# The steps' softplus chunk by chunk in the state-space stage of a perceiver kernel

## The reference, cut to what matters

```
ssm = x @ W_x.T
ts, Bm, Cm = (ssm[..., :R], ssm[..., R:R + N], ssm[..., R + N:])
ts = rms_forward(ts); Bm = rms_forward(Bm); Cm = rms_forward(Cm)
dt = jax.nn.softplus(ts @ W_dt.T + b_dt)
A = -jnp.exp(A_log)
def step(state, inp):
    dA = jnp.exp(dt_t[..., None] * A)
    state = state * dA + (dt_t * u_t)[..., None] * B_t[:, None, :]
    y = jnp.einsum('bdn,bn->bd', state, C_t)
```

## Time and profile before

| | us |
|---|---|
| median of three runs (2577.83 to 2579.14) | 2577.83 |
| the profiled execution, its device time | 2577.61 |
| its span, first to last instruction | 2575.7 |
| TensorE busy in the span | 2475.4 (96%) |
| VectorE busy | 1857.3 (72%) |
| ScalarE busy | 1525.6 (59%) |
| GpSimd busy | 1464.5 (57%) |

### The profile page before, as it was taken

One profiled execution on the slowest core, in us unless ns is written; L12 is line 12 of the kernel. 1 busy time (PEld: TensorE's weight loads), 2 busy tenths in 40 slices (PEclk: granted clock), 3 DMA queues, 4 the chain that ended last, 5 costly groups with the idle time before them and its releaser, 6 DMA issues. The chain is left out here.

```text
span 2575.7 us, 42761 instructions
## 1 busy us (share of the span) xinstructions
PE 2475.4 (96%) x16984; PEld 2271.0 (88%) x16984; DVE 1857.3 (72%) x2085; ACT 1525.6 (59%) x2605; POOL 1464.5 (57%) x1201
## 2 busy tenths in 40 slices
PE   8999999999999999999999999999999699899889
PEld 6899999999999999999999999999887477754557
DVE  4157787787877788778877778877746699843573
ACT  3356665676566666667666566665643577622672
POOL 3345686586666568657666756865700499400452
PEclk9999999999999999999999999999999799999889
DMA  6511011111111101112111120111251300188200
GB/s 224 193 60 54 29 62 54 43 59 54 37 49 46 62 29 62 54 36 66 54 37 38 50 68 29 62 29 33 102 188 54 131 1 1 54 315 310 84 2 17
DMA packets 112238, 188.70 MB, mean 73 GB/s; under 512 B 9940, under 2 KB 74836, under 8 KB 110252
## 3 DMA queue, kind: packets, MB, share of 16 engines
q1 hardware_dynamic: 103724, 177.64, 20.6%
q10 hardware_dynamic: 8320, 8.39, 1.0%
HBM read 165.98 MB, written 20.02 MB: 72 GB/s over the span
## 5 line engine op out<-in xcount | busy, mean ns | idle before, releaser
L513 POOL TENSOR_TENSOR xa_pt_lo<-xs_st,xa_pt_hi 128x1024 fp32r<-128x1024 f32 x191 | 468.4, 2484 | 466.3 <-ACT xa_pt_hi L767 466.3
L59 PE MATMUL ctx_kv_ps<-ctx_wv_hi,ctx_hi 128*128 128x256 f32 x1536 | 431.7, 281 | 1.8 <-DVE xa_v_lo L880 1.8
L60 PE MATMUL ctx_kv_ps<-ctx_wv_lo,ctx_hi 128*128 128x256 f32 x1536 | 430.0, 280 | 0.0
L61 PE MATMUL ctx_kv_ps<-ctx_wv_hi,ctx_lo 128*128 128x256 f32 x1536 | 429.9, 280 | 0.0
L59 PE MATMUL ctx_kv_ps<-ctx_hi,ctx_wk_hi 128*128 128x402 f32 (+1 forms) x1024 | 357.3, 349 | 1.8 <-DVE xa_k_lo L873 1.8
L60 PE MATMUL ctx_kv_ps<-ctx_lo,ctx_wk_hi 128*128 128x402 f32 (+1 forms) x1024 | 353.2, 345 | 0.0
L61 PE MATMUL ctx_kv_ps<-ctx_hi,ctx_wk_lo 128*128 128x402 f32 (+1 forms) x1024 | 353.0, 345 | 0.0
L59 PEld LDWEIGHTS ctx_kv_ps<-ctx_wv_hi,ctx_hi 128*128 128x128 f32 x1536 | 288.6, 188 | 2.2 <-DVE xa_v_lo L880 2.2
L60 PEld LDWEIGHTS ctx_kv_ps<-ctx_wv_lo,ctx_hi 128*128 128x128 f32 x1536 | 289.4, 188 | 0.0
L61 PEld LDWEIGHTS ctx_kv_ps<-ctx_wv_hi,ctx_lo 128*128 128x128 f32 x1536 | 288.5, 188 | 0.0
L744 ACT ACTIVATE xs_st<-xs_s_ps 128x512 f32<-128x512 f32 (+1 forms) x448 | 263.3, 604 | 29.1
(11 more groups left out here) (531 smaller groups left out, 6765.8 us busy)
## 6 DMA issues: line engine op xcount, KB each, us to landing
ctx_raw<-in_ctx_t SPq DMA_DIRECT2D x24, 804.0 KB, 6.9
ctx_wk_raw<-in_xa_wk SPq DMA_DIRECT2D x64, 256.0 KB, 2.8
ctx_wv_raw<-in_xa_wv SPq DMA_DIRECT2D x32, 512.0 KB, 4.4
n_back<-in_ctx SPq DMA_DIRECT2D x8, 1280.0 KB, 10.4
q_raw<-in_xa_wq SPq DMA_DIRECT2D x8, 1024.0 KB, 4.9
q_scratch<-q_q_sb ACTq DMA_DIRECT2D x8, 1024.0 KB, 4.4
ctx_q_raw<-q_scratch SPq DMA_DIRECT2D x64, 128.0 KB, 2.7
o_scratch<-xa_o_sb SPq DMA_DIRECT2D x64, 128.0 KB, 1.7
```

The source lines that it names most:

```text
L59: nc.tensor.matmul(out, left[0], right[0], start=first, stop=False)
L60: nc.tensor.matmul(out, left[0], right[1], start=False, stop=False)
L61: return nc.tensor.matmul(out, left[1], right[0], start=False, stop=last)
L513: nc.gpsimd.tensor_tensor(by_chunk(pt_lo, p), scored(j, p).rearrange("p g q c -> p g c q"), by_chunk(pt_hi, p).bitcast(F32), ALU.subtract) ...
```

## The change

The logarithm of chunk c - 2 is issued behind the exponential of chunk c - 1, inside the loop over the chunks; the addition of chunk c - 4 is issued in VectorE's loop at chunk c; the exponential of A_log is issued at chunk 1, and its negation at chunk 4. One logarithm of a 128 x 1 tile (`logs`) is new, ahead of the loop.

```diff
-        eps_sb = sc.sb("eps", [P, 1])
+        eps_sb, logs = sc.sb("eps", [P, 1]), sc.sb("logs", [P, 1])
...
+            def step_sum(c):
+                dve.wait_ge(d_read, c + 1)
+                dve.wait_ge(ln_set, c + 1)
+                nc.vector.tensor_tensor(dt_sb[:, c, :], dt_sb[:, c, :], work[:, c, :], ALU.add).then_inc(dt_set, 1)
+
             for c in range(DC):
                 if folded_pair(c):
                     for n in range(HN):
...
                 dve.wait_ge(d_abs, c + 1)
                 nc.vector.tensor_scalar(work[:, c, :], d_ps[:, c % 4, :], bd[:, c:c + 1], 0.0,
                                         ALU.add, ALU.max).then_inc(d_read, 1)
-            for c in range(DC):
-                dve.wait_ge(d_read, c + 1)
-                dve.wait_ge(ln_set, c + 1)
-                nc.vector.tensor_tensor(dt_sb[:, c, :], dt_sb[:, c, :], work[:, c, :], ALU.add).then_inc(dt_set, 1)
-            dve.wait_ge(a_exp, 1)
-            nc.vector.tensor_scalar(a_sb[:, :, :], a_sb[:, :, :], -1.0, None, ALU.mult)
+                if c == 4:
+                    dve.wait_ge(a_exp, 1)
+                    nc.vector.tensor_scalar(a_sb[:, :, :], a_sb[:, :, :], -1.0, None, ALU.mult)
+                if c > 3:
+                    step_sum(c - 4)
+            for c in range(DC - 4, DC):
+                step_sum(c)
...
             nc.scalar.activation(steps_t[:, :], t_ps[0:COPIES * RANK, :], ACT.Copy).then_inc(steps_set, 1)
+            nc.scalar.activation(logs[:, :], eps_sb[:, :], ACT.Ln, bias=1.0)
             act.wait_ge(small_in, (COPIES + 1) * 16)
 
             def decline(c):
                 act.wait_ge(d_abs, c + 1)
                 nc.scalar.activation(dt_sb[:, c, :], dt_sb[:, c, :], ACT.Exp, scale=-1.0).then_inc(e_set, 1)
 
+            def logarithm(c):
+                act.wait_ge(e_set, c + 1)
+                nc.scalar.activation(dt_sb[:, c, :], dt_sb[:, c, :], ACT.Ln, bias=1.0).then_inc(ln_set, 1)
+
             for c in range(DC):
                 act.wait_ge(d_full, c + 1)
                 nc.scalar.activation(dt_sb[:, c, :], d_ps[:, c % 4, :], ACT.Abs, bias=bd[:, c:c + 1]).then_inc(d_abs, 1)
+                if c == 1:
+                    act.wait_ge(scan_in, 32)
+                    nc.scalar.activation(a_sb[:, :, :], a_sb[:, :, :], ACT.Exp).then_inc(a_exp, 1)
                 if c > 0:
                     decline(c - 1)
+                if c > 1:
+                    logarithm(c - 2)
             decline(DC - 1)
-            for c in range(DC):
-                act.wait_ge(e_set, c + 1)
-                nc.scalar.activation(dt_sb[:, c, :], dt_sb[:, c, :], ACT.Ln, bias=1.0).then_inc(ln_set, 1)
-            act.wait_ge(scan_in, 32)
-            nc.scalar.activation(a_sb[:, :, :], a_sb[:, :, :], ACT.Exp).then_inc(a_exp, 1)
+            logarithm(DC - 2)
+            logarithm(DC - 1)
```

## The result

| | before | changed |
|---|---|---|
| median of five runs, us | 2577.95 | 2590.67 |
| range of the runs, us | 2577.83 to 2579.14 | 2589.76 to 2596.11 |
| profiled execution: device time, span | 2577.61, 2575.7 | 2595.96, 2594.0 |

The change makes the kernel 12.7 us slower by the medians. The ratio goes by all runs and not by the two medians: it is 1.0055, with a 95% interval of 1.0044 to 1.0066, and the means of the five and five runs are 14.3 us apart. The forecast was 2592.8 in a range of 2589 to 2597.

The account below looks back on a forecast made before the run. VectorE's end, behind ScalarE's chain, was taken to bound the steps' stage. The stage 14.5 us longer plus 0.5 at the scan's start made 15.0 us, so 2592.8 us, range 2589 to 2597.

Parts of the forecast that it names:

- cost at the scan's start: Load between the zeros' copy and the scan's exponentials: first scan 2.96 instead of 2.45 us behind GpSimd's product, 0.5 more.
- small logarithm on the path: New small logarithm and its load, some 1.28 + 0.2 us, lie in ScalarE's 2.22 us wait for the first product: cost 0.
- What a load costs: Each table load in a row of ScalarE's work costs 1.41 us, with 1.28 as the lower end.
- The stage: The steps' stage, up to GpSimd's first scan product, becomes 14.5 us longer, with ScalarE's last logarithm late at the end.
- The gain of the order by itself: In the steps' stage and scan's start, interleaving by itself gains about 3.3 us against 18.3 for added loads.
- that one sentence: Sum counted by loads: 13 more on the path at 1.41 make 18.3 us, and interleaving by itself gains about 3.3.
- Behind it the scan should read as before: After the first scan, nothing takes the delay in and the scan's profile stays as before.
- rival 3: TensorE's clock changes VectorE's 2.58 us wait in the scan: coming twice 2595.4 us, removed 2590.2; 9% together.
- Rivals 1 and 2: 1: one table set serves both functions, 2575.1 us, 3%; 2: alternating tables cost a second pause per load, 2609.4 us, 2%.

Follow-up runs that it names:

- the pairs: Changed kernel with its loop's logarithms issued in pairs at chunks 3, 5 and 7, 27 table loads instead of 33: median 2584.34 us, ratio 1.0022.
- the kernels with one table: Logarithms replaced by same-shape exponentials, 18 table loads: in the changed kernel ratio 0.9988, in the kernel before 0.9997, there with the table loaded early 0.9985.
- the changed order with one table: Changed kernel with its eight logarithms and the small new one replaced by exponentials, 18 table loads instead of 33: median 2575.63 us, ratio 0.9988.
- the order of before with A_log's part alone: Kernel before with only A_log's exponential moved to chunk 1 and its negation to VectorE's chunk 4: median 2577.78 us, ratio 0.9997.
- the second comparison: The changed kernel run once more, unaltered, beside new runs of the kernel before: median 2594.02 us, ratio 1.0056.

## Why the prediction was right

Its steps against the profile, counted from the first absolute value:

| step | predicted | measured |
|---|---|---|
| loads in the stage, at the scan's start | 16, 1 | 16, 1 |
| from one logarithm to the next | 4.44 | 4.46 |
| last logarithm ends | 33.04 | 33.14 |
| last addition ends | 33.99 | 34.01 |
| GpSimd's first product of the scan | 34.32 | 34.37 |
| first scan | 37.28 | 37.25 |
| cost at the scan's start | 0.51 | 0.43 |
| small logarithm on the path | 0 | 0 (0.71 us of the wait left) |

*What a load costs.* 1.41 us was taken from two places of the trace of before; six loads less in the pairs gave 1.42, and the load ahead of the additions 1.43. That the built program's loads are what runs was the step on which the sign hung, and the kernels with one table show that it is these loads and nothing else in the new order.

*The stage.* +14.50 predicted, 34.37 - 19.87 = +14.50 measured. The gain of the order by itself was put at 3.3 us as a remainder of the sum. The experiments give the interleaving itself nothing (19.66 against 19.71). The remainder is two other things. VectorE ended 3.64 us behind the last logarithm before (2043.59 against 2039.95) and ends 0.87 behind it now, so that 2.8 us of ScalarE's longer chain cost nothing; and the scan's load costs 0.43 instead of 1.41. The 0.2 of A_log's exponential goes the other way. The sum was right, since it walked ScalarE's chain from start to end and did not multiply loads; that one sentence in it was not. On VectorE two details were wrong and cost nothing: beside GpSimd's product a chunk's diagonal matrices, maximum and addition take 1.90 + 0.75 + 0.68 = 3.33 us and not under 3, of the 4.46 there are; and VectorE waits ahead of its maxima, not ahead of most additions.

*Behind the scan's start.* "Behind it the scan should read as before" did not hold, and it is the one step that failed: 1.0 us comes back there. SyncE's transfer at the start of the next stage:

```profile
2240.24 0.33 SPq L2285 DMA_DIRECT2D mo_raw<-in_fl_w  x1
```

From the first value to it it takes 214.82 us against 200.91 before, +13.91, while the first scan stood at +14.93. All of it comes back by the seventh scan, which starts 17.28 us behind the first instead of 18.27. The second scan before, then in the changed kernel:

```profile
2048.68 2.30 DVE L2042 TENSOR_TENSOR_SCAN ms_h_ps<-ms_h_ps,mamba_a_d_bu 128x1024 f32<-128x1024 f32 x1
```

```profile
2064.88 2.27 DVE L2055 TENSOR_TENSOR_SCAN ms_h_ps<-ms_h_ps,mamba_a_d_bu 128x1024 f32<-128x1024 f32 x1
```

Before, the second and third scan start 2.31 us apart, at the pace of GpSimd's products (2.32 each). Now the first scan has waited longer for ScalarE, GpSimd is ahead, and they start 2.21 and 2.18 apart. So 0.23 of the 0.43 us that the load costs at the scan's start are given back at once. The rest is VectorE's wait ahead of the seventh scan, 1.84 us instead of 2.58, and it goes with the granted clock. Before (two stretches, the first scan at 2046.37):

```profile
2050.00:2056.00 6.00, 3.35 (x14) 2.44 (x13) 5.99 (x4) 3.99 (x8) 6.00 (x4) 0.50 0.06 25
2056.00:2060.00 4.00, 4.00 (x26) 3.48 (x25) 4.00 (x3) 2.16 (x4) 4.00 (x2) 0.75 0.00 0
```

And changed (the first scan at 2062.67):

```profile
2066.00:2072.00 6.00, 3.61 (x15) 2.69 (x14) 6.00 (x4) 3.95 (x8) 6.00 (x4) 0.50 0.06 22
2072.00:2074.00 2.00, 2.00 (x14) 1.64 (x13) 2.00 (x2) 1.97 (x4) 2.00 (x2) 0.87 0.00 0
```

The mean of 0.75 over four us before puts the rise from 1.2 to 2.4 GHz near 2058, 11.6 us behind the first scan; the mean of 0.87 over two us puts it near 2072.5 now, 9.8 behind. This is the better half of rival 3, which expected up to 2.6 us. The first turnings at the lower level are the same in both (1.97 us), so the difference lies in when the rise comes. The same reading of all eleven profiles goes with this, though no run moves the rise by itself: the rise comes 9.8 to 12.4 us behind the first scan and the seventh scan 17.3 to 18.7 us behind it, and where the one is later, so is the other (a single pair of neighbours is exchanged, by 0.11 us). Whether the change moves the rise is open. The changed kernel has it at 9.8 and 10.0 in its two profiles, but the changed order with one table, which idles less than before, has it at 10.2, and the order of before with A_log's part alone at 10.7. So it varies without the loads too.

*The median.* 15.0 us were predicted. The first comparison has 12.7 by the medians and 14.3 by the means; the second has 15.0 by the medians (2594.02 less 2579.00) and 14.4 by its ratio of 1.0056. With the 13.9 us between the first value and the next stage all of these agree within the spread of the runs, which in the changed kernel reaches 6.4 us. So the times of whole runs don't confirm the sum to better than some 2 us, and that the second comparison hits it is luck; what bears it out is the table above. The profiled execution was forecast at 2592.6 and took 2595.96, 18.35 us more than before: 1.37 stand ahead of the first value, 13.91 between it and the next stage, and 3.01 behind (347.59 against 344.58), which the second profile of the same kernel (344.34) does not show. The lower bound of the range was added up wrongly: 2590.6 less rival 3's 2.6 is 2588.0, not 2588.9. The measured median lies above both.

*Rivals 1 and 2.* With exponential and logarithm in turn each needed its own load, so one table did not serve both. The Trainium skill (ScalarE: Activation LUTs, Table sets: the hidden batching unit) has a set with both of them, for one load; the trace does not agree, since in this built program each switch has its own. Whether that set exists and was not chosen, no run here shows. No load had a second pause behind it in the stage, in this kernel or in those of the experiments (0.01 to 0.02 us between a load in a row of work and its activation); the drain of 1380 ns in the Trainium skill (ScalarE: Activation LUTs, What ACT_TABLE_LOAD costs) shows in none.

## What to carry to other kernels

Before two functions are interleaved on ScalarE, count the table loads in the built program, which the source does not show, and price each by its place: about 1.4 us where ScalarE's chain sets the end, 0.4 at the scan's start beside GpSimd's product, nothing where ScalarE waits or where another engine is later. If a chain of several functions is the bound, look for a formula with fewer of them before reordering: here, with z small enough for it, it gained 8.0 us of the stage and 6 to 8 of the whole (the ratio and the medians), and the new order without any of its extra loads gained nothing over the old one.

## What the runs showed of the hardware

- A table load takes 1283 ns in every group of all eleven profiles, whatever it follows, and alternating at a distance of 2 us makes it no longer.
- VectorE's work on SBUF stretches while GpSimd multiplies dt and u beside it, diagonal matrices too: a group of four took 1.90 us instead of about 1. Beside GpSimd's own diagonal matrices a group takes 0.98 to 1.03 in the kernel before, and 0.86 when GpSimd has finished them (at 2032.32). GpSimd's product of dt and u was 1.26 us beside VectorE's diagonal matrices, against 1.66 (3.32 for two) beside the additions of before.
- The granted clock of TensorE rose from 0.50 to 1.00 between 9.8 and 12.4 us behind the first scan, in eleven profiles with the same instructions from there on, and the seventh scan moved with it by up to 1.4 us.
- In the last stages it differs between two executions of one program (0.91 against 0.98 in one stretch); the way from the next stage to the output took 3.25 us longer in the first.
